# The pieces of x go to their partitions by DMA instead of by picks on the matrix engine

## The chip, the cores and the metric

One Trainium2 chip, one core of it. The metric is the device time of one launch in microseconds (us). The kernel before was timed three times, and once more under the profiler. TensorE (PE) multiplies, VectorE (DVE), ScalarE (ACT) and GpSimd (POOL) work on tiles in the on-chip memory, and SP issues most DMAs.

## The reference, cut to what matters

`x` is 64 x 64 x 512 (batch, time, features), the initial state `cond` 64 x 512. A GRU runs over the 64 time steps, and a feed-forward layer in emulated 8-bit floats follows.

```
def cell(h, x):
    gi = x @ W_ih + b_ih
    gh = h @ W_hh + b_hh
    i_r, i_z, i_n = jnp.split(gi, 3, axis=-1)
    h_r, h_z, h_n = jnp.split(gh, 3, axis=-1)
    r = jax.nn.sigmoid(i_r + h_r)
    z = jax.nn.sigmoid(i_z + h_z)
    n = jnp.tanh(i_n + r * h_n)
    h_new = (1.0 - z) * n + z * h
    return (h_new, h_new)
...
t = jax.nn.silu(g) * u
qt, st, sct = _reorder_quantize_x(t, down_reorder_index)
y = _qlinear(qt, st, sct, w_down, down_reorder_index)
...
x = x + ffn(gru(cond, x))
```

The recurrence is very sensitive to rounding in its first steps, so the kernel computes these with sums in an emulated order.

## The kernel before

**Stages.** A set-up splits the weights into half-precision kinds and writes them to DRAM (`w_rows`), to about 203 us of the span. Six *emulated* steps follow, to about 2,270 us, and then 58 plain steps with the feed-forward layer.

**Products.** The emulated steps are a list, `PRODUCTS`, of ten products (t, m): m = 0 is x of step t times W_ih, m = 1 the state times W_hh. The order is (0,0), (0,1), (1,0), (1,1), (2,0), (2,1), (3,0), (3,1), (4,1), (5,1); i is the place in it. Each has 32 blocks (`NBK`) of 16 rows of the contraction. For t < 2 a product is *fine* (`fine_chain`, 384 matmuls of 32 columns a block, two buffers, `PAIR`), after that a *sum* product (`sum_chain`, 64 matmuls a block, four buffers, `BUFS`). All of a product is added in the banks `run[m]`; `run_ok[1]` counts the blocks done, and with it everyone knows which buffer is free (`emptied`).

**What a product needs.** VectorE cuts the turned operand into six kinds of pieces (`cut_pieces`, into `a_split`). TensorE *picks* (L967): matmuls with the selection matrices `low_sel` and `whole_sel` bring rows of `a_split` to the partitions where the chain wants them, 8 groups of 10 matmuls in a fine product and of 8 in a sum product. ScalarE (`place`) and VectorE (`place_second`) copy the results into `low_a` and `whole_a`, one buffer for x and state alike. From these GpSimd (`one_hots`, L741 and L747), or ScalarE in (2,0) and (3,0) (`x_one_hots`, L833), makes a block's operands `whole_hot` and `low_hot`. SP loads a block's weights (`weights`, L687 and L694): 4 DMAs, in a fine product 12. In a fine product VectorE and ScalarE also rebase `whole_w` between blocks (L1047, L815), and for block 0 set it to zero (L1040, L822).

**Order around the change.** On TensorE a product is: in a state product the turn of the state (L948), two matmuls that clear `run[m]` (L955), the picks, then the chain. In an x product the cut was made during the state product ahead of it. SP waits before `weights(i)` until all blocks of the product before are done:

```
sp.wait_ge(run_ok[1], block_no(i, 0) + BUFS)
blocks(sp, i, load)
```

VectorE runs `elementwise(t - 1)`, the gates of the last step, during x product (t,0): in (1,0) woven between its rebasing, ten instructions a block, in (2,0) and (3,0) in one go. All loops of SP, GpSimd and ScalarE over blocks have one body for `bufs(i)` blocks, so two or four.

Of the kernel before, what the change touches and what calls it, by code (L numbers as in the profile page):

```python
# [11 lines left out]
F16 = mybir.dt.float16  # L12
# [71 lines left out]
def build(nc, x, cond, w_ih, w_hh, b_ih, b_hh, w_gate, w_up, w_down, up_idx, dn_idx, out):  # L84
# [14 lines left out]
    with ctx:  # L99
# [37 lines left out]
        with ExitStack() as ex:  # L137
# [112 lines left out]
            with ExitStack() as sx:  # L250
# [23 lines left out]
                id_z = ssem("id_z")  # L274
# [28 lines left out]
                with nc.Block() as block:  # L303
# [29 lines left out]
                    @block.gpsimd  # L333
                    def _(pool):
                        nc.gpsimd.memset(ex_ident[:], 0.0).then_inc(id_z, 1)
                        pool.wait_ge(id_z, 1)
# [46 lines left out]
                    def _(v):  # L383
# [18 lines left out]
                        v.wait_ge(id_ok, 1)  # L402
# [82 lines left out]
                    @block.tensor  # L485
                    def _(pe):
                        pe.wait_ge(id_ok, 1)
# [24 lines left out]
                        pe.wait_ge(plain_ok, 2)  # L512
                        x_pairs(pe, range(SETUP_PAIRS), raw, SETUP_BANKS)

            with ExitStack() as sx:
# [8 lines left out]
                low_a = ssb("low_a", [P, NBK, SUBS, B], F16)  # L524
                whole_a = ssb("whole_a", [P, NBK, B], F16)
# [9 lines left out]
                w_x = ssb("w_x", [P, KD, G3])  # L535
                COUNT_AT = 2
# [21 lines left out]
                placed_second = ssem("placed_second")  # L558
                w_in = [ssem(f"w_in{b}") for b in range(BUFS)]
# [35 lines left out]

                def places(i):

                    return 2 * PB if fine(i) else PB

# [24 lines left out]
                def blocks(eng, i, block, first=0):  # L624

                    for c in range(first):
                        block(c, c % bufs(i))
                    with eng.Fori(first // bufs(i), NBK // bufs(i)) as n:
                        for b in range(bufs(i)):
                            block(n * bufs(i) + b, b)  # L630
# [13 lines left out]
                with nc.Block() as block:  # L644
                    @block.sync
                    def _(sp):
# [29 lines left out]
                        def weights(i):  # L676
                            m = PRODUCTS[i][1]

                            def load(c, buf):

                                sp.wait_ge(run_ok[1], emptied(i, c))
# [16 lines left out]
                            sp.wait_ge(run_ok[1], block_no(i, 0) + BUFS)  # L698
                            blocks(sp, i, load)
# [27 lines left out]
                    def _(pool):  # L727
# [3 lines left out]
                        def one_hots(i):  # L731
                            m = PRODUCTS[i][1]

                            def make(c, buf):

                                pool.wait_ge(placed[m], placed_by(i) + placed_for(i, c))
                                pool.wait_ge(placed_second, second_by(i) + placed_for(i, c))
                                pool.wait_ge(hot_ok, block_no(i, c) + 1)
                                pool.wait_ge(run_ok[1], emptied(i, c))
                                if fine(i):  # L740
                                    nc.gpsimd.tensor_tensor(  # L741
                                        whole_hot[:, buf].rearrange("p s k c -> p (s k) c"),
                                        whole_a[:, bass.ds(c, 1), :].to_broadcast([P, 2 * BK, B]),
                                        whole_mask[:].rearrange("p s k -> p (s k)").unsqueeze(2).to_broadcast([P, 2 * BK, B]),
                                        ALU.mult).then_inc(whole_ok, 1)
                                    pool.wait_ge(whole_ok, block_no(fine_no(i), c) + 1)
                                nc.gpsimd.tensor_tensor(  # L747
                                    low_hot[:, buf].rearrange("p (s k) b -> p s k b", s=SUBS),
                                    low_a[:, bass.ds(c, 1), :, :].rearrange("p a s b -> p (a s) b").unsqueeze(2).to_broadcast([P, SUBS, SK, B]),
# [3 lines left out]
                            blocks(pool, i, make, FIRST)  # L753
# [14 lines left out]
                    def _(a):  # L768
                        for part in range(2):
                            own = slice(part * B, part * B + Q)  # L770
                            for bq in range(2):
                                nc.scalar.activation(whole_a[own, :, bq * Q:(bq + 1) * Q], ex_ident[own, own].unsqueeze(1).to_broadcast([Q, NBK, Q]),
                                                     ACT.Copy, scale=HIGH_ONE)
# [21 lines left out]
                        def place(i):  # L795
                            m = PRODUCTS[i][1]
                            for n in range(places(i)):
                                a.wait_ge(selected[m], placed_by(i) + n + 1)
                                group, whole = pick_of(i, n)
                                if whole:  # L800
                                    last = nc.scalar.activation(whole_a[Q:2 * Q, group::PB, :], picked(n, slice(Q, 2 * Q)), ACT.Copy)
                                else:
                                    for part in range(2):
                                        last = nc.scalar.activation(low_a[part * B:(part + 1) * B, group::PB, 0, :], picked(n, slice(0, B)), ACT.Copy)  # L804
# [21 lines left out]
                        def x_one_hots(i):  # L826
                            def make(c, buf):

                                a.wait_ge(placed_second, second_by(i) + places(i))
                                a.wait_ge(hot_ok, block_no(i, c) + 1)  # L830
                                a.wait_ge(run_ok[1], emptied(i, c))
                                for k in range(SK):
                                    last = nc.scalar.activation(low_hot[:, buf, k::SK, :],  # L833
                                                                low_a[:, bass.ds(c, 1), :, :].rearrange("p a s b -> p (a s) b"),
# [3 lines left out]
                            blocks(a, i, make)  # L838

                        for i, (t, m) in enumerate(PRODUCTS):  # L840
# [12 lines left out]
                    def _(pe):  # L853
# [97 lines left out]
                        def pick(i):  # L951
                            t, m = PRODUCTS[i]
                            need(pe, gates_ok[m], t * 2)
                            for u in range(2):
                                nc.tensor.matmul(run[m][u], zeros[:], zero_row[:], start=True, stop=True, skip_group_check=True)  # L955
                            pe.wait_ge(a_split_ok[m], t + 1)
# [38 lines left out]
                    def _(v):  # L995
# [3 lines left out]
                        def cut_pieces(t, m):  # L999
# [7 lines left out]
                            v.wait_ge(turned[m], t + 1)  # L1007
                            yield link(vs(a_rest[:, m], ps_a_both[m].rearrange("p (j s b) -> p s j b", j=2, s=2),
# [17 lines left out]
                        def place_second(i):  # L1026
                            m = PRODUCTS[i][1]
                            for n in range(places(i)):
                                v.wait_ge(selected[m], placed_by(i) + n + 1)
                                group, whole = pick_of(i, n)  # L1030
                                if whole:
                                    last = nc.vector.tensor_copy(whole_a[B + Q:2 * B, group::PB, :], picked(n, slice(B + Q, 2 * B)))
                                else:
                                    for part in range(2):
                                        last = nc.vector.tensor_copy(low_a[part * B:(part + 1) * B, group::PB, 1, :], picked(n, slice(B, 2 * B)))  # L1035
# [368 lines left out]
        with ExitStack() as sx:  # L1404
# [14 lines left out]
            ident_z = ssem("ident_z")  # L1419
# [23 lines left out]
            with nc.Block() as block:  # L1443
# [15 lines left out]
                def _(pool):  # L1459
                    nc.gpsimd.memset(ident[:], 0.0).then_inc(ident_z, 1)  # L1460
                    pool.wait_ge(ident_z, 1)
# [13 lines left out]
                def _(v):  # L1475
                    nc.vector.memset(zero16[:], 0.0).then_inc(zero_ok, 1)
                    v.wait_ge(ident_ok, 1)
# [723 lines left out]
```

## Time and profile before

| | us |
|---|---|
| timed runs | 3220.37, 3244.61, 3233.75 |
| their median | 3233.75 |
| the profiled execution | 3218.36 |
| its span | 3216.5 |
| mean granted clock of TensorE | 0.944 |

The span is the time between the first and the last instruction of the profiled execution. The profile has busy time by engine, the span in 40 slices (one is 80.4 us), DMA queues, the chain of work that ended last, and groups of instructions by line. A timeline row gives the start in us from the span's start, the duration, engine, line, operation, output and inputs, count, and in brackets the idle time of the engine before it and what ended that. `PEld` is TensorE loading weights, `SPq` a DMA issued by SP. Matmuls overlap, so the duration of one is far above its share.

### The profile page before, as it was taken

Reading aid. Unit: us, or ns where it says so; the run is one execution under the profiler, and the core shown is the slowest. Engines: PE = TensorE matmul, PEld = TensorE weight load, DVE = VectorE, ACT = ScalarE, POOL = GpSimd, SP = SyncE. Lnnn points to the kernel's source line nnn. Section 1 sums busy time; section 2 is a strip of 40 time slices with the busy share of each in tenths; the row PEclk is TensorE's granted clock in tenths of the full one; section 3 lists DMA queues with packets and bytes.
Section 4 is the critical chain, followed back from the end, with each engine's and each line's share of the span. In section 5 each row is a group of like instructions: output and inputs, shape, how many; then the busy total and the mean of one; then the engine's idle time right before and its main releaser. Section 6 shows DMA issues by size and latency. Waiting matters only on the chain. (4 is left out here: it accounts for less than half of the span.)

```text
span 3216.5 us, 156784 instructions
## 1 busy us (share of the span) xinstructions
PE 2801.9 (87%) x67963; PEld 1888.0 (59%) x67963; DVE 1808.8 (56%) x3503; ACT 1176.6 (37%) x2417; POOL 1249.5 (39%) x640
## 2 busy tenths in 40 slices
PE   5649999999999899999999999999941599999996
PEld 2227886888678677887767764646410244444442
DVE  6533423342369842523757427081767488888887
ACT  2332212222212122223806413030245377777774
POOL 1226554565455445553060341606020133333333
PEclk9869999999999999999999999999965799999998
DMA  6752222222122122222544452424240223222321
GB/s 173 173 145 65 62 65 54 60 66 62 50 59 59 53 61 53 63 62 66 151 135 123 123 146 79 141 102 122 88 153 25 92 78 91 85 83 84 90 72 48
DMA packets 214339, 286.43 MB, mean 89 GB/s; under 512 B 49197, under 2 KB 174151, under 8 KB 214023
## 3 DMA queue, kind: packets, MB, share of 16 engines
q1 hardware_dynamic: 194791, 235.99, 26.4%
q10 hardware_dynamic: 13568, 33.56, 2.9%
q0 software_dynamic: 5856, 15.22, 2.4%
q8 instruction: 78, 1.28, 0.2%
q14 instruction: 46, 0.38, 0.0%
HBM read 226.10 MB, written 58.48 MB: 88 GB/s over the span
## 5 line engine op out<-in xcount | busy, mean ns | idle before, releaser
L865 PE MATMUL psum<-whole_w,whole_hot 64*32 64x384 f16 x32768 | 1199.6, 325 | 38.5 <-issue 16.3
L873 PE MATMUL psum<-low_w,low_hot 64*32 64x384 f16 x16384 | 1004.1, 325 | 3.8 <-issue 3.8
L865 PEld LDWEIGHTS psum<-whole_w,whole_hot 64*32 64x32 f16 x32768 | 741.6, 93 | 192.6 <-DVE whole_w L1047 51.2
L747 POOL TENSOR_TENSOR low_hot<-low_a,sum_mask 128x1024 f16<-128x1024 f16 x256 | 485.2, 1895 | 537.7 <-DVE low_a L1035 434.0
L741 POOL TENSOR_TENSOR whole_hot<-whole_a,whole_mask 128x2048 f16<-128x2048 f16 x128 | 462.4, 3612 | 570.4 <-PE psum L865 502.9
L1047 DVE TENSOR_SCALAR whole_w<-psum 32x384 f16<-32x384 f32 x496 | 272.2, 549 | 691.9 <-PE psum L865 683.7
L815 ACT ACTIVATE whole_w<-psum 32x384 f16<-32x384 f32 x496 | 239.3, 483 | 960.3 <-PE psum L865 957.4
L935 PE MATMUL psum<-low_w,low_hot 64*64 64x384 f16 x12288 | 506.6, 324 | 9.5 <-ACT low_hot L833 7.9
L935 PEld LDWEIGHTS psum<-low_w,low_hot 64*64 64x64 f16 x12288 | 374.9, 108 | 140.3 <-ACT low_hot L833 8.4
L873 PEld LDWEIGHTS psum<-low_w,low_hot 64*32 64x32 f16 x16384 | 404.9, 93 | 59.2 <-issue 8.5
L1822 PE MATMUL psum<-wh,hT 128*64 128x256 f32 (+1 forms) x1856 | 315.0, 492 | 0.0
L2017 POOL TENSOR_TENSOR store<-store 128x512 f32<-128x512 f32 (+1 forms) x96 | 156.4, 1658 | 337.7 <-ACT store L1938 337.6
L231 PE MATMUL psum<-w_x,x_cols 128*64 128x256 f32 (+1 forms) x1408 | 237.0, 496 | 7.4 <-ACT x_cols L201 7.4
L1822 PEld LDWEIGHTS psum<-wh,hT 128*64 128x64 f32 x1856 | 128.9, 138 | 181.4 <-issue 156.2
L1843 PE MATMUL psum<-qgu,store 128*128 128x512 f16 (+1 forms) x768 | 173.1, 370 | 36.4 <-DVE store L2087 28.3
L1093 DVE SCALAR_TENSOR_TENSOR ex_gates_h<-psum,unscale,bias 128x384 f32<-128x384 f32 x12 | 7.0, 615 | 312.8 <-PE psum L935 297.8
L231 PEld LDWEIGHTS psum<-w_x,x_cols 128*64 128x64 f32 x1408 | 100.7, 139 | 137.6 <-issue 107.7
L833 ACT ACTIVATE low_hot<-low_a,sum_scale 128x128 f16 x512 | 156.6, 388 | 9.3 <-DVE low_a L1035 1.1
L195 ACT ACTIVATE psum<-bias_sum 128x512 f32<-128x512 f32 x58 | 34.8, 600 | 284.9 <-DVE ex_gates_h L1093 251.4
L1843 PEld LDWEIGHTS psum<-qgu,store 128*128 128x128 f16 x768 | 69.5, 99 | 116.5 <-issue 26.6
L804 ACT ACTIVATE low_a<-psum 64x256 f16<-64x256 f32 x160 | 60.2, 376 | 200.1 <-PE psum L967 195.5
L1566 PE MATMUL psum<-ident,q 128*128 128x128 f16 x132 | 18.8, 309 | 117.7 <-DVE q L1502 117.7
(265 smaller groups left out, 3126.2 us busy)
## 6 DMA issues: line engine op xcount, KB each, us to landing
low_w<-w_rows SPq DMA_DIRECT2D x384, 144.0 KB, 2.4
low_w<-w_rows SPq DMA_DIRECT2D x256, 120.0 KB
whole_w<-w_rows SPq DMA_DIRECT2D x1024, 24.0 KB, 1.8
x_gates<-x_out ACTq DMA_DIRECT2D x58, 384.0 KB, 2.4
xg<-x_gates SPq DMA_DIRECT2D x58, 384.0 KB, 3.2
low_w<-w_rows SPq DMA_DIRECT2D x256, 72.0 KB
low_w<-w_rows SPq DMA_DIRECT2D x384, 48.0 KB, 2.2
w_rows<-w_split SPq DMA_DIRECT2D x64, 144.0 KB
```

Of the source, the lines that this page charges most:

```text
L231: last = nc.tensor.matmul(banks[1][n % 2][part][half * B:(half + 1) * B, :], lhs, parts(w, k, half)[part], start=False, stop=True, skip_gr ...
L741: nc.gpsimd.tensor_tensor(whole_hot[:, buf].rearrange("p s k c -> p (s k) c"), whole_a[:, bass.ds(c, 1), :].to_broadcast([P, 2 * BK, B]), ...
L747: nc.gpsimd.tensor_tensor(low_hot[:, buf].rearrange("p (s k) b -> p s k b", s=SUBS), low_a[:, bass.ds(c, 1), :, :].rearrange("p a s b -> p ...
L815: last = nc.scalar.activation(whole_w[u * B:u * B + Q, buf, 1, bq, :], run[m][u][(2 + bq) * Q:(3 + bq) * Q, :], ACT.Copy, scale=1.0 / HIGH ...
L833: last = nc.scalar.activation(low_hot[:, buf, k::SK, :], low_a[:, bass.ds(c, 1), :, :].rearrange("p a s b -> p (a s) b"), ACT.Copy, scale= ...
L865: last = nc.tensor.matmul(run[m][u][j * Q:(j + 1) * Q, :], whole_hot[rows[u], buf, sign, kk, j % 2 * Q:(j % 2 + 1) * Q], whole_w[rows[u], ...
L873: nc.tensor.matmul(run[m][u][j * Q:(j + 1) * Q, :], low_hot[rows[u], buf, kk, j % 2 * Q:(j % 2 + 1) * Q], low_w[rows[u], buf, at:at + UC], ...
L935: last = nc.tensor.matmul(run[m][u][half * B:(half + 1) * B, :], low_hot[own, buf, kk, :], low_w[own, buf, at:at + UC], start=False, stop= ...
L1047: last = nc.vector.tensor_scalar(whole_w[u * B:u * B + Q, c % PAIR, 0, bq, :], run[m][u][bq * Q:(bq + 1) * Q, :], 1.0 / HIGH_ONE, None, AL ...
L1822: last = nc.tensor.matmul(dst, lhs, w, start=False, stop=True, skip_group_check=True)
L1843: last = nc.tensor.matmul(dst[:, 0:w], qhT[:, k, :], qgu[:, k, base + o:base + o + w], start=k == 0, stop=k == KD - 1)
L2017: nc.gpsimd.tensor_tensor(t_t[:, s], u_t[:, s], silu_t[:, s], ALU.mult).then_inc(t_ok, 1)
```

## The change

The x products of steps 1 to 3 get no picks and no copies. Their pieces are written to DRAM (`x_pieces`) and read from there into the partitions, by DMA, while the state product ahead of them runs: in (0,1) and (1,1) by SP, with the write ahead of the last eight blocks' weights and the reads spread over these; in (2,1) by ScalarE at its start. `low_a` and `whole_a` exist twice, for x and for the state, and their layout has the group outside. The picks of (0,0) and of all state products stay.

Three things go with it. SP's wait for the whole product ahead is replaced by a wait for each buffer (`opened`). The loops over blocks have one body for eight (`PB`) blocks. Two semaphores of the identity matrices are merged into others.

```diff
+                def regrouped(i):
+                    return i > 0 and bufs(i) != bufs(i - 1)
+
+                def opened(eng, i, c):
+                    eng.wait_ge(run_ok[1], emptied(i, c))
+                    if regrouped(i) and isinstance(c, int) and c < PAIR:
+                        eng.wait_ge(run_ok[1], block_no(i, 0) + BUFS - PAIR + 1 + c)
+
+                def by_dma(i):
+                    t, m = PRODUCTS[i]
+                    return m == 0 and t > 0
+
                 def places(i):
+                    if by_dma(i):
+                        return 0
                     return 2 * PB if fine(i) else PB
+
+                def pieces_of_x(t):
+                    t_fine = t < X_FINE
+                    kinds = LOW_ROWS if t_fine else SUM_ROWS
+                    low = [(part * B + row * SK, kind, None) for part in range(2) for row, kind in enumerate(kinds)]
+                    whole = [(part * B + Q + (sub * WHOLE_KINDS + row) * SK, kind, sub)
+                             for part in range(2) for sub in range(SUBS) for row, kind in enumerate(WHOLE_ROWS)]
+                    return low + whole if t_fine else low
+
+                def move_x(eng, piece):
+                    to, kind, sub = piece
+                    if sub is None:
+                        eng.dma_start(low_a[0][to:to + SK].rearrange("k q s g b -> k (q s) (g b)"),
+                                      x_pieces[kind].rearrange("(n k) c -> k n c", k=SK)).then_inc(moved_x, 16)
+                    else:
+                        eng.dma_start(whole_a[0][to:to + SK].rearrange("k q g b -> k q (g b)"),
+                                      x_pieces[kind].rearrange("(q s k) c -> s k q c", s=SUBS, k=SK)[sub]).then_inc(moved_x, 16)
+
+                def put_x(eng, t):
+                    eng.wait_ge(a_split_ok[0], t + 1)
+                    need(eng, moved_x, moved_by(t - 1))
+                    eng.dma_start(x_pieces[:].rearrange("j p c -> p j c"),
+                                  a_split[:, :, 0:KD, :].rearrange("p j g b -> p j (g b)")).then_inc(put, 16)
+                    eng.wait_ge(put, 16 * t)
...
-                        for b in range(bufs(i)):
-                            block(n * bufs(i) + b, b)
+                        for b in range(PB):
+                            block(n * PB + b, b % bufs(i), n, b)
...
-                            sp.wait_ge(run_ok[1], block_no(i, 0) + BUFS)
-                            blocks(sp, i, load)
+                            if not pieces:
+                                blocks(sp, i, load, 1 if regrouped(i) else 0)
+                                return
+                            blocks(sp, i, load, end=KD - 1)
+                            put_x(sp, t + 1)
+                            for c in range(NBK - PB, NBK):
+                                load(c, c % bufs(i), c // PB, c % PB)
+                                for piece in pieces[c % PB * share:(c % PB + 1) * share]:
+                                    move_x(sp, piece)
...
                             elif m == 0:
-                                a.wait_ge(placed[0], placed_by(i) + places(i))
                                 x_one_hots(i)
+                            elif t + 1 < X_SUMS:
+                                a.wait_ge(hot_ok, block_no(i, 0) + 1)
+                                put_x(a, t + 1)
+                                for piece in pieces_of_x(t + 1):
+                                    move_x(a, piece)
...
                                 nc.tensor.matmul(run[m][u], zeros[:], zero_row[:], start=True, stop=True, skip_group_check=True)
+                            if by_dma(i):
+                                return
```

On TensorE, between the chain of (0,1) and that of (1,0), the program before stands so (`low_sel` and `whole_sel` are the selection matrices):

```order
L897 COMPARE_AND_BRANCH
L955 MATMUL psum<-zero_row,zeros 128x384 x2
L967 MATMUL psum<-a_split,low_sel 128x256 x8
L967 MATMUL psum<-a_split,whole_sel 128x256 x2
...
L967 MATMUL psum<-a_split,whole_sel 128x256 x2
L897 UNCONDITIONAL_BRANCH
L897 ISA
L906 ISA
L865 MATMUL psum<-whole_w,whole_hot 32x384 x4
```

and that of the change so:

```order
L964 REGISTER_ALU
L964 COMPARE_AND_BRANCH
L1022 MATMUL psum<-zero_row,zeros 128x384 x2
L964 UNCONDITIONAL_BRANCH
L964 ISA
L973 ISA
L932 MATMUL psum<-whole_w,whole_hot 32x384 x4
```

Of the work between the chains only the two clears are left; at (2,0) and (3,0) it is the same.

On SP, in (0,1), from the end of its loop over 24 blocks on, the program of the change has:

```order
L678 COMPARE_AND_BRANCH
L646 DMA x_pieces<-a_split 128x6x256
L739 DMA low_w<-w_rows 40x2x768
L739 DMA low_w<-w_rows 24x2x768
L746 DMA whole_w<-w_rows 16x2x384 x4
L739 DMA low_w<-w_rows 40x2x768
L739 DMA low_w<-w_rows 24x2x768
L746 DMA whole_w<-w_rows 16x2x384 x4
L636 DMA low_ax<-x_pieces 8x16x256 x3
```

The write of the pieces stands ahead of block 24's weights, and three reads stand behind each block's twelve DMAs.

## Rows read from the trace of the kernel before

**Rows 1.** The page: busy time by engine; instruction queues: packets, MB

```profile
PE 2801.9 (87%) x67963; PEld 1888.0 (59%) x67963; DVE 1808.8 (56%) x3503; ACT 1176.6 (37%) x2417; POOL 1249.5 (39%) x640
...
q8 instruction: 78, 1.28, 0.2%
```

**Rows 2.** Timeline, start of (1,0): start us, us, engine, line, operation, tiles, count, idle before

```profile
846.97 0.50 PE L955 MATMUL psum<-zero_row,zeros 128*128 128x384 f16 x2
...
847.72 0.89 DVE L1040 MEMSET whole_w<- 32x384 uint32 x2
...
859.17 1.89 ACT L822 ACTIVATE whole_w<-zero_row 32x384 f16<-32x384 f16 x4
...
860.31 0.34 PE L865 MATMUL psum<-whole_w,whole_hot 64*32 64x384 f16 x4 [2.12 <-ACT whole_w L822]
```

**Rows 3.** Timeline, start of (2,0)

```profile
1511.26 7.15 PE L967 MATMUL psum<-a_split,low_sel 128*128 128x256 f16 x64
...
1522.35 1.17 PE L935 MATMUL psum<-low_w,low_hot 64*64 64x384 f16 x11 [3.94 <-ACT low_hot L833]
```

**Rows 4.** Timelines, start of (3,0) and its end

```profile
1705.90 5.31 PE L935 MATMUL psum<-low_w,low_hot 64*64 64x384 f16 x69 [1.34 <-issue]
...
1711.47 7.15 PE L967 MATMUL psum<-a_split,low_sel 128*128 128x256 f16 x64
...
1722.55 0.86 PE L935 MATMUL psum<-low_w,low_hot 64*64 64x384 f16 x8 [3.93 <-ACT low_hot L833]
...
1807.31 0.20 PEld L948 LDWEIGHTS psum<-ex_ident,a_in 128*128 128x128 f32 x2 [0.30 <-issue]
```

**Rows 5.** Windows: us, busy time and instructions of each engine, granted clock, DMA share, GB/s

```profile
861.00:871.00 10.00, 10.00 (x372) 8.25 (x364) 0.97 (x2) 1.02 (x3) 0.50 (x1) 0.83 0.02 5
1522.00:1532.00 10.00, 9.65 (x176) 7.08 (x180) 10.00 (x27) 9.46 (x32) 0.00 (x0) 0.72 0.19 57
1704.00:1716.00 12.00, 10.42 (x128) 7.55 (x121) 4.45 (x10) 3.01 (x8) 0.00 (x0) 1.00 0.23 50
1722.00:1732.00 10.00, 9.45 (x200) 7.19 (x204) 10.00 (x28) 9.47 (x32) 0.00 (x0) 0.83 0.23 66
```

**Rows 6.** Timelines of SP's queue (fine, start of (2,0), set-up); page: DMA issues to landing

```profile
791.66 0.79 SPq L687 DMA_DIRECT2D low_w<-w_rows  x2
...
800.92 0.79 SPq L687 DMA_DIRECT2D low_w<-w_rows  x2
...
804.80 1.79 SPq L694 DMA_DIRECT2D whole_w<-w_rows  x4
...
1511.35 9.75 SPq L687 DMA_DIRECT2D low_w<-w_rows  x16
...
58.04 117.48 SPq L308 DMA_DIRECT2D w_rows<-w_split  x48
...
low_w<-w_rows SPq DMA_DIRECT2D x384, 48.0 KB, 2.2
```

**Rows 7.** Timeline, ScalarE's one-hots in (2,0)

```profile
1519.77 15.35 ACT L833 ACTIVATE low_hot<-low_a,sum_scale 128x128 f16 x48 [0.56 <-DVE low_a L1035]
```

**Rows 8.** Timelines: ScalarE's start; VectorE's gates at the end of (2,0)

```profile
203.36 1.06 ACT L772 ACTIVATE whole_a<-ex_ident 32x1024 f16<-32x1024 f32 x1 [17.03 <-PEq L303]
...
216.30 0.76 ACT L804 ACTIVATE low_a<-psum 64x256 f16<-64x256 f32 x2 [8.93 <-PE psum L967]
...
1608.31 1.14 DVE L1093 SCALAR_TENSOR_TENSOR ex_gates_x<-psum,unscale,bias 128x384 f32<-128x384 f32 x2 [15.20 <-PE psum L935]
```

**Rows 9.** Timeline, GpSimd's one-hots in (1,0)

```profile
1083.20 3.60 POOL L741 TENSOR_TENSOR whole_hot<-whole_a,whole_mask 128x2048 f16<-128x2048 f16 x1 [3.85 <-PE psum L865]
1086.98 1.89 POOL L747 TENSOR_TENSOR low_hot<-low_a,sum_mask 128x1024 f16<-128x1024 f16 x1 [0.17 <-POOL whole_hot L741]
...
1125.28 3.61 POOL L741 TENSOR_TENSOR whole_hot<-whole_a,whole_mask 128x2048 f16<-128x2048 f16 x1 [4.68 <-PE psum L865]
```

**Rows 10.** DMA queues over 1080 to 1115: instruction packets, MB

```profile
q8 instruction: 9, 0.15, 2.0%
```

More of the change, by code:

```diff
@@ L535, in build @@
                 w_x = ssb("w_x", [P, KD, G3])
+                x_pieces = nc.dram_tensor("x_pieces", [A_KINDS, P, KD * B], F16, kind="Internal").ap()
                 COUNT_AT = 2
@@ L622, in emptied, with blocks @@
                     return block_no(i, c) + BUFS - bufs(i) + 1
[L624 to L628, printed above, removed]
-                        for b in range(bufs(i)):
-                            block(n * bufs(i) + b, b)
+                def blocks(eng, i, block, first=0, end=KD):
+                    for c in range(first * PB):
+                        block(c, c % bufs(i), c // PB, c % PB)
+                    with eng.Fori(first, end) as n:
+                        for b in range(PB):
+                            block(n * PB + b, b % bufs(i), n, b)
                 def placed_for(i, c):
@@ L676, in weights, with load @@
                         def weights(i):
-                            m = PRODUCTS[i][1]
-                            def load(c, buf):
-                                sp.wait_ge(run_ok[1], emptied(i, c))
+                            t, m = PRODUCTS[i]
+                            pieces = pieces_of_x(t + 1) if fine(i) and m == 1 and t + 1 < X_SUMS else ()
+                            share = -(-len(pieces) // PB)
+                            def load(c, buf, gk, group):
+                                opened(sp, i, c)
                                 src = w_rows[bass.ds(c + m * NBK, 1)].rearrange("a r n -> r (a n)")
@@ L731, in one_hots, with make @@
                         def one_hots(i):
[L732 to L737, printed above, removed]
+                            t, m = PRODUCTS[i]
+                            def make(c, buf, gk, group):
+                                if by_dma(i):
+                                    pool.wait_ge(moved_x, moved_by(t))
+                                else:
+                                    pool.wait_ge(placed[m], placed_by(i) + placed_for(i, c))
+                                    pool.wait_ge(placed_second, second_by(i) + placed_for(i, c))
                                 pool.wait_ge(hot_ok, block_no(i, c) + 1)
-                                pool.wait_ge(run_ok[1], emptied(i, c))
+                                opened(pool, i, c)
                                 if fine(i):
@@ L748, in make @@
                                     low_hot[:, buf].rearrange("p (s k) b -> p s k b", s=SUBS),
-                                    low_a[:, bass.ds(c, 1), :, :].rearrange("p a s b -> p (a s) b").unsqueeze(2).to_broadcast([P, SUBS, SK, B]),
+                                    low_a[m][:, group, :, bass.ds(gk, 1), :].rearrange("p s a b -> p (s a) b").unsqueeze(2).to_broadcast([P, SUBS, SK, B]),
                                     sum_mask[:].unsqueeze(1).unsqueeze(3).to_broadcast([P, SUBS, SK, B]),
                                     ALU.mult).then_inc(hot_ok, 1)
-                            blocks(pool, i, make, FIRST)
+                            blocks(pool, i, make, 0 if by_dma(i) else 1)
                         for i, (t, m) in enumerate(PRODUCTS):
@@ L800, in place @@
                                 if whole:
[L801 removed]
+                                    last = nc.scalar.activation(whole_a[m][Q:2 * Q, group, :, :], picked(n, slice(Q, 2 * Q)), ACT.Copy)
                                 else:
                                     for part in range(2):
[L804 removed]
+                                        last = nc.scalar.activation(low_a[m][part * B:(part + 1) * B, group, 0, :, :], picked(n, slice(0, B)), ACT.Copy)
                                 last.then_inc(placed[m], 1)
@@ L826, in x_one_hots, with make @@
                         def x_one_hots(i):
-                            def make(c, buf):
-                                a.wait_ge(placed_second, second_by(i) + places(i))
+                            def make(c, buf, gk, group):
+                                a.wait_ge(moved_x, moved_by(PRODUCTS[i][0]))
                                 a.wait_ge(hot_ok, block_no(i, c) + 1)
-                                a.wait_ge(run_ok[1], emptied(i, c))
+                                opened(a, i, c)
                                 for k in range(SK):
                                     last = nc.scalar.activation(low_hot[:, buf, k::SK, :],
-                                                                low_a[:, bass.ds(c, 1), :, :].rearrange("p a s b -> p (a s) b"),
+                                                                low_a[0][:, group, :, bass.ds(gk, 1), :].rearrange("p s a b -> p (s a) b"),
                                                                 ACT.Copy, scale=sum_scale[:, k:k + 1])
                                 last.then_inc(hot_ok, 1)
-                            blocks(a, i, make)
+                            blocks(a, i, make, 1 if regrouped(i) else 0)
                         for i, (t, m) in enumerate(PRODUCTS):
```

38 lines of the change are left out of this document (22 added, 16 removed).

## The prediction

> **What bounds the kernel now.** I read the page first. TensorE is busy 87% of the span, VectorE 56%, the others less [rows 1], so I take TensorE's matmul chains as the bound of the emulated steps, and what can be won there is time in which no chain runs. Next I read the timeline at the three places where the change takes the picks out, the starts of products (1,0), (2,0) and (3,0).
>
> - (1,0) [rows 2]: the two clears start at 846.97, the picks follow, and the chain starts at 860.31. Its last releaser is ScalarE's zero of `whole_w` (L822), which stands behind its copies of the picks.
> - (2,0): picks from 1511.26 for 7.15 us and the chain at 1522.35 after 3.94 us idle [rows 3]; ScalarE, which copies first, starts the one-hots only at 1519.77 [rows 7].
> - (3,0) [rows 4]: picks from 1711.47, chain at 1722.55, the same shape.
>
> At the starts of the state products the picks cannot go (they wait for the new state), and the change leaves them. Last I read the windows for the granted clock [rows 5], because after the idle ahead of each of these chains it falls: 0.83 over 861 to 871, 0.72 over 1522 to 1532, 0.83 over 1722 to 1732.
>
> **The change, part by part.** *Picks removed.* What could hold the new chain start?
>
> (1,0): run banks are cleared at once. The first base needs VectorE's memset, which starts at 847.72 right behind the gate values and takes 0.89 for two [rows 2], so the first is there at about 848.17. ScalarE's zeros no longer have copies ahead of them and lie under the last block. From the end of two zeros (859.17 + 0.94 = 860.11) to the chain (860.31) is 0.20. So the chain could start at 848.37 instead of 860.31: **11.94 us**. It needs block 0's one-hots and weights by then. GpSimd takes 3.6 + 1.9 = 5.5 us for a block [rows 9], SP 5.7 us to issue (800.92 to 806.59) and the last DMA some 2.2 us to land [rows 6], 7.9 in all; both may start when block 30 of the product before is done, one block, 9.26 us, ahead of the end (SP's rhythm: 791.66, 800.92). Covered, by 1.4 us. Block 1's have the whole of block 0.
>
> (2,0): no base is needed. The chain could start where the first pick did, 1511.26, instead of 1522.35: **11.09 us**. ScalarE makes a block in 8 x 0.32 = 2.6 us (48 in 15.35, [rows 7]) and has block 0's one-hots and SP its weights during the last fine block. Block 1 is late: its buffer was in use by the last fine block, so SP opens it at about 1511.0, its four DMAs go out as block 0's did from 1511.35, at 0.6 each (16 in 9.75, [rows 6]), the fourth at about 1513.1, and lands 2.2 later, 1515.3 to 1515.4. TensorE wants it at 1511.26 + 2.65 = 1513.9 (product (3,0) runs 32 blocks from 1722.55 to 1807.31, [rows 4]). A new wait of **1.5 us**; blocks 2 and 3 follow at 2.4 us each and are in time. Net 9.6.
>
> (3,0): four buffers before and after, so everything for blocks 0 to 3 is loaded and made during the last four blocks of (2,1). 1711.47 instead of 1722.55: **11.08 us**.
>
> *Clock.* The shortfalls of [rows 5] are 0.17 x 10 + 0.28 x 10 + 0.17 x 10 = 6.2 us of work at full clock. They go if the idle that came before them goes. What is left is 0.9 us at (1,0) and 1.5 at (2,0). The nearest row is an idle of 1.34 us that ended at 1705.90 [rows 4], after which the clock over 1704 to 1716 stayed 1.00. I take the whole **6.2**; the other end is 1.7, (3,0) alone, which has no idle left.
>
> *DMAs added.* In (0,1) SP writes `x_pieces` once ahead of its last eight blocks, waits for it, and issues 24 moves, three a block; in (1,1) 16, two a block; in (2,1) ScalarE issues 16, which has nothing else to do there between its copies and the next product. In a fine product SP has 9.26 - 5.7 = 3.6 us free a block. The lower end of an issue is 0.4 us (two in 0.79, [rows 6]): 1.2 a block, hidden by that idle. The upper end is the writes of the set-up, 48 in 117.48 or 2.45 each, with their waits for VectorE in it [rows 6]: three make 7.35, 3.8 too late a block. A move has 128 or 64 short rows, near `low_w` (40x2 and 24x2) and `whole_w` (16x2) in kind and far from the set-up, where SP waits for VectorE's splitting; so I take 0.4 and nothing. The write moves 384 KB. At the 2.2 us of a load it is there as block 24 opens, since SP reaches it 5.7 us after block 21's end and has 3.6 left: nothing, and up to 2 us once a product if its many short rows take twice that. The last move of (0,1) is issued behind block 31's weights: that block opens 18.5 us ahead of the end, so 18.5 - 5.7 - 1.2 = 11.6 ahead, and at 2.2 us to land the pieces are there 9.4 ahead, where GpSimd may start at 9.26 and has 3.8 us to spare.
>
> *Copies moved.* `low_a` is laid out by group; the one-hot instructions keep count and size, so nothing. Four more 1 us activations at the start (L772, four from 203.36 on) end before 212, ScalarE's first copy is at 216.30 [rows 8]: hidden by the wait for the pieces. `elementwise` in (2,0) starts earlier by the copies that VectorE loses, about 7 us, while the chain ends some 11 earlier: the 15.20 us that VectorE waited at its end [rows 8] shrink by 4, and nothing waits for it. VectorE's weave in (1,0), which stretches that product, is unchanged.
>
> Sum: 11.94 + 9.6 + 11.08 + 6.2 = **38.8 us**. The profiled execution took 3218.36, so 3179.6 on its terms. The three timed ones were 3220.37, 3244.61 and 3233.75, median 15.4 above it; the mean of the four is 3229.3. I forecast on the mean: 3229.3 - 38.8 = 3190.5, say **3190**. On the median it would be 3195.
>
> **Code loading** is the term I can't place. In (1,0) GpSimd's whole one-hots, one a block, start at 1083.20 and, three blocks on, at 1125.28 [rows 9] where 9.26 apart is the rule: 42.1 us, 14.3 lost, and in that stretch nine packets of instructions were loaded on TensorE's queue [rows 10], of 78 in the whole span [rows 1]. It happened in mid-loop, where the code had been there before. The change moves all code behind (0,1), so this may vanish (3176) or come twice (3205); both ends go into the range.
>
> The Trainium skill (Runtime: NRT & Kernel Launch, Instruction fetch mechanics) says that a taken branch to code outside a small window must fetch it first, and gives 32 KiB as the store of most engines. The row that bears on it: 78 instruction packets, 1.28 MB, for TensorE's 135,926 instructions [rows 1], under ten bytes each, so most trips of the loops loaded nothing. By the rule taken strictly, loops of eight blocks could load each trip; by the row, they don't. This is the last rival below.
>
> **Rivals.**
> 1. *Forecast*, 0.62: the three heads go.
> 2. *The head is hidden behind something else*, 0.18: the first block's weights, one-hots or code are late at each new start. For it: the cover at (1,0) is 1.4 us. If each start waits 4 us and the clock falls as before: 11.94 + 9.6 + 11.08 - 12 + 0 = 20.6 saved, 3209. Within 1%.
> 3. *SP is late in the state products*, 0.14: moves at 2.45. Then 3.8 x 8 in (0,1) and (2 x 2.45 - 3.6) x 8 = 10.4 in (1,1), 40.8 lost, 3231. Within 1%. It decides from 1.2 us an issue on. Against it: SP's issues are even throughout these stretches.
> 4. *Slower*, 0.06: the loops of SP, GpSimd and ScalarE, two or four blocks long and now eight, load code on each trip. SP makes 4 + 3 + 4 + 3 = 14 trips in fine products. At the 14.3 us that one reload of TensorE's cost, 200 - 38.8 = 161 more, 3390. It decides from (38.8 + 32.3) / 14 = 5.1 us a trip. Against it: [rows 1] as above.
>
> **How the numbers follow.** Within 1% (32.3 us of 3233.75) is about what a measurement of this kernel can tell from no change; faster means below 3201.4. Rival 1 has its ends at 3176 and 3205, of which about one part in ten lies above the bound; rival 2 may land either side with the executions' own spread of 24 us. Faster 0.60, same 0.34, slower 0.06. The range is from 3166 (no reload, on the profiled execution's terms: 3179.6 - 14.3 = 3165.3) to 3219 (rival 2's 3209 and ten of the executions' 24 us).
>
> **What would show it.** No `low_sel` or `whole_sel` matmul between the clears and the chain at the three places; the first chain matmul within 1.5 us of the clears; a wait of about 1.5 us at block 1 of (2,0); clock 1.00 in the first 10 us of (3,0); SP's weight issues 9.26 apart in the last eight blocks of (0,1). Wrong: blocks of GpSimd's more than 9.5 apart there, idle of TensorE over 2 us at the new starts, or many more instruction packets than 78 on TensorE's queue or SP's rhythm broken at a loop's turn.

## The result, and the profile after

The changed kernel takes 3183.05 us, median of four runs (3173.21 to 3186.78), against 3228.12 for the kernel before (four runs, 3220.37 to 3244.61): ratio 0.9849, 95% interval 0.9802 to 0.9896, or 45 us less. The forecast was 3190 (3166 to 3219). The profiled execution took 3183.72, 34.6 less than the profiled one before. The medians below leave out three executions that lay in the slow state: 4285.13 us of before_padded, 3254.72 and 6509.78 us of after_padded87.

The page of the changed kernel, as in [rows 1]:

```profile
span 3181.9 us, 155502 instructions
...
PE 2773.8 (87%) x67755; PEld 1877.9 (59%) x67755; DVE 1784.3 (56%) x3447; ACT 1159.3 (36%) x2365; POOL 1247.0 (39%) x640
...
q8 instruction: 67, 1.10, 0.1%
```

The 208 picks and 56 copies of VectorE are gone, and 11 packets of code of the queue q8 (which I take for TensorE's: nine of them come while its loop stands still), of which more below. The starts of the three products are in the timeline of the changed kernel, against [rows 2 to 4]:

```profile
846.56 0.50 PE L1022 MATMUL psum<-zero_row,zeros 128*128 128x384 f16 x2
...
847.31 0.89 DVE L1111 MEMSET whole_w<- 32x384 uint32 x2
...
847.79 0.34 PE L932 MATMUL psum<-whole_w,whole_hot 64*32 64x384 f16 x4 [0.73 <-DVE whole_w L1111]
...
1487.08 0.50 PE L1022 MATMUL psum<-zero_row,zeros 128*128 128x384 f16 x2
...
1487.50 2.79 PE L1002 MATMUL psum<-low_w,low_hot 64*64 64x384 f16 x64
1491.23 4.06 PE L1002 MATMUL psum<-low_w,low_hot 64*64 64x384 f16 x93 [0.94 <-issue]
...
1685.64 0.50 PE L1022 MATMUL psum<-zero_row,zeros 128*128 128x384 f16 x2
...
1686.07 2.14 PE L1002 MATMUL psum<-low_w,low_hot 64*64 64x384 f16 x48
```

The chain follows its clears by 1.2 us in (1,0), where it waits for VectorE's memset, and by 0.4 in the others; in (2,0) block 1 waits 0.94 for its weights. The windows behind the three starts, against [rows 5], have the full clock:

```profile
848.00:858.00 10.00, 8.80 (x367) 7.04 (x363) 1.30 (x3) 0.97 (x2) 4.32 (x2) 1.00 0.23 59
1487.00:1497.00 10.00, 9.06 (x214) 7.02 (x214) 9.69 (x33) 9.48 (x32) 0.00 (x0) 1.00 0.55 152
...
1686.00:1696.00 10.00, 10.00 (x245) 7.16 (x248) 9.89 (x33) 8.94 (x30) 0.00 (x0) 1.00 0.52 147
```

To see where the time went I took the times between the first clears of successive products, from the timelines of all traces (us; "rest" is all behind the clears of (5,1)). These stretches differ between executions too, "rest" by up to 9 us over all traces:

| trace | to (0,0) | (0,0) | (0,1) | (1,0) | (1,1) | (2,0) | (2,1) | (3,0) | (3,1) | (4,1) | rest |
|---|---|---|---|---|---|---|---|---|---|---|---|
| before | 209.8 | 320.3 | 316.9 | 343.3 | 320.6 | 97.6 | 102.7 | 96.5 | 181.6 | 180.9 | 1046.5 |
| changed | 211.5 | 319.6 | 315.4 | 320.2 | 320.3 | 85.2 | 113.4 | 84.0 | 182.0 | 181.1 | 1049.2 |

Three stages pay: (1,0) -23.1, (2,0) -12.4, (3,0) -12.5. Everything else is within 3 us but (2,1), which is **10.7 longer**. The trace shows why. ScalarE's queue, TensorE, and the windows there:

```profile
1595.80 0.40 ACTq L646 DMA_DIRECT2D x_pieces<-a_split  x1
1599.83 14.22 ACTq L636 DMA_DIRECT2D low_ax<-x_pieces  x16
```

```profile
1589.75 18.53 PE L1002 MATMUL psum<-low_w,low_hot 64*64 64x384 f16 x452
1613.70 6.57 PE L1002 MATMUL psum<-low_w,low_hot 64*64 64x384 f16 x120 [5.42 <-issue]
```

```profile
1598.00:1603.00 5.00, 5.00 (x132) 3.60 (x124) 4.86 (x9) 0.00 (x0) 3.79 (x2) 1.00 0.99 228
1603.00:1608.00 5.00, 5.00 (x132) 3.54 (x124) 4.89 (x6) 0.00 (x0) 3.78 (x2) 1.00 1.05 139
1608.00:1613.00 5.00, 0.28 (x8) 0.00 (x0) 4.89 (x7) 0.00 (x0) 1.89 (x1) 1.00 1.09 129
1613.00:1618.00 5.00, 4.30 (x72) 3.05 (x76) 4.89 (x7) 0.00 (x0) 0.00 (x0) 0.66 0.57 127
```

Two windows of (2,1) in the kernel before, for comparison:

```profile
1625.00:1660.00 35.00, 35.00 (x868) 25.22 (x864) 34.02 (x45) 0.00 (x0) 24.72 (x13) 1.00 0.49 139
1660.00:1711.00 51.00, 49.42 (x1168) 34.98 (x1156) 0.31 (x2) 0.00 (x0) 28.51 (x16) 1.00 0.51 124
```

The sixteen reads of step 3's pieces go out at once, the DMA engines are full (share about 1.0, where the stage before had 0.5), TensorE stops 5.42 us, for which the profile names no releaser, and comes back at a clock of 0.66. A second stop of 2.23 us ends at 1,628.02. The two stops and the clock (0.34 x 5 = 1.7) are 9.4 of the 10.7. The DMA view of 1,598 to 1,613, then the page's issues over the whole kernel, show weights that land late:

```profile
low_w<-w_rows SPq DMA_DIRECT2D x11, 144.0 KB, 4.4
```

```profile
low_w<-w_rows SPq DMA_DIRECT2D x384, 144.0 KB, 2.5
```

A load of 144 KB lands 4.4 us after its issue instead of 2.5, and a block of a sum product lasts 2.6. That is the median; the load that TensorE needed was later still. In the trace's semaphore records TensorE's queue waits from 1,607.50 for 6.14 us, and one of its two conditions is the semaphore of that block's weights. SP had issued these from 1,600.96 to 1,602.47, and their last landing stands at 1,613.61, 11 us after the last issue. The stop ends at 1,613.70.

### The profile page after: what moved, and what is told of

It reads as the page before. It is cut to its first block and busy times, and to the rows that moved or that the text cites. A ratio compares the mean times of both kernels' runs of the same rounds, so it can differ in the third digit from the quotient of the medians.

```text
span 3181.9 us, 155502 instructions
## 1 busy us (share of the span) xinstructions
PE 2773.8 (87%) x67755; PEld 1877.9 (59%) x67755; DVE 1784.3 (56%) x3447; ACT 1159.3 (36%) x2365; POOL 1247.0 (39%) x640
## 5 line engine op out<-in xcount | busy, mean ns | idle before, releaser
L809 POOL TENSOR_TENSOR low_hot<-low_ah,sum_mask 128x1024 f16<-128x1024 f16 x192 | 363.7, 1894 | 514.6 <-DVE low_ah L1106 411.1
L1002 PEld LDWEIGHTS psum<-low_w,low_hot 64*64 64x64 f16 x12288 | 383.4, 107 | 132.3 <-issue 12.4
L803 POOL TENSOR_TENSOR whole_hot<-whole_ah,whole_mask 128x2048 f16<-128x2048 f16 x64 | 231.1, 3610 | 274.2 <-PE psum L932 237.0
L803 POOL TENSOR_TENSOR whole_hot<-whole_ax,whole_mask 128x2048 f16<-128x2048 f16 x64 | 231.1, 3611 | 270.2 <-PE psum L932 256.1
L896 ACT ACTIVATE low_hot<-low_ax,sum_scale 128x128 f16 (+1 forms) x512 | 156.6, 388 | 104.9 <-PE psum L1002 85.8
L809 POOL TENSOR_TENSOR low_hot<-low_ax,sum_mask 128x1024 f16<-128x1024 f16 x64 | 121.3, 1895 | 10.3 <-POOL whole_hot L803 9.7
```

Source lines behind the costliest of these rows:

```text
L803: nc.gpsimd.tensor_tensor(whole_hot[:, buf].rearrange("p s k c -> p (s k) c"), whole_a[m][:, group, bass.ds(gk, 1), :].to_broadcast([P, 2 ...
L809: nc.gpsimd.tensor_tensor(low_hot[:, buf].rearrange("p (s k) b -> p s k b", s=SUBS), low_a[m][:, group, :, bass.ds(gk, 1), :].rearrange("p ...
L896: last = nc.scalar.activation(low_hot[:, buf, k::SK, :], low_a[0][:, group, :, bass.ds(gk, 1), :].rearrange("p s a b -> p (s a) b"), ACT.C ...
L1002: last = nc.tensor.matmul(run[m][u][half * B:(half + 1) * B, :], low_hot[own, buf, kk, :], low_w[own, buf, at:at + UC], start=False, stop= ...
```

## The experiments

The first four ran on one chip with the kernel before (3226.75 us there), the next four on one (3229.04), the last four on one (3222.47).

**after_again** is the changed kernel once more.

> The changed kernel once more, as the yardstick of this chip and for a second trace. In its first trace product (2,1), from its clears to those of (3,0), took 113.7 us where the kernel before took 102.9, and TensorE sat idle 5.4 us at 1,608. Theory A (ScalarE's burst of sixteen reads takes the DMA engines from the weights, share 1.0 over 1,598 to 1,613): the same stretch takes 112 to 115 us again, with the idle within 10 us of the burst. Theory B (chance, like a code load): it takes about 103. Product (1,0) took 320.0 us from clears to the turn of (1,1), before 343.0, of which 14.3 was a code load in mid-loop: if that load is chance by execution, (1,0) may take 334 here; if it belongs to the layout of the code, 320 again.

3183.97 us, ratio 0.9863 (0.9803 to 0.9922). (2,1) took 110.7, a little under the 112 expected, with the stop again behind the burst. The burst began 7 us later this time, and the stop 9:

```profile
1606.62 14.41 ACTq L636 DMA_DIRECT2D low_ax<-x_pieces  x16
...
1622.43 7.79 PE L1002 MATMUL psum<-low_w,low_hot 64*64 64x384 f16 x152 [4.77 <-issue]
```

The queue waits here from 1,616.48 for 5.90 us; the last landing of the block's weights stands at 1,622.34. Chance (B) is out. (1,0) took 325.5, between the two values expected, but again with 6 packets of code: the reload of [rows 9, 10] doesn't come back.

**paced** spreads the burst.

```diff
-                                for piece in pieces_of_x(t + 1):
+                                for n, piece in enumerate(pieces_of_x(t + 1)):
+                                    a.wait_ge(hot_ok, block_no(i, 4 + 3 * n // 2) + 1)
                                     move_x(a, piece)
```

> The changed kernel with the sixteen reads of (2,1) paced: one for each block and a half, each behind a wait for GpSimd's one-hots of block 4 + 3n/2, instead of all in one go. Theory A (the burst starves the weights): (2,1) takes 103 to 105 us instead of 113.7, (3,0) starts as early as now, and the kernel is 9 to 11 us faster than the changed one, near 3172. Theory C (the 16 reads cost DMA time however they are spread, since the weights need 0.6 of the engines already): (2,1) takes 109 or more. Theory B (chance): no difference.

3176.39 us, ratio 0.9853 (0.9792 to 0.9914); (2,1) took 106.4, and its longest stop in the chain is 0.8 us. Both are short of what was expected (103 to 105, near 3172). The burst is the cause of 4 to 7 us. Up to 3.7 are left over the stage before, and the DMA share over the spread reads is 0.76:

```profile
1604.31 48.79 ACTq L636 DMA_DIRECT2D low_ax<-x_pieces  x16
```

```profile
1618.00:1660.00 42.00, 41.66 (x1020) 36.31 (x1016) 9.14 (x14) 0.00 (x0) 30.13 (x17) 1.00 0.76 170
```

**x3_picks** gives step 3 its picks back, so (2,1) has no moves.

```diff
-                    return m == 0 and t > 0
+                    return m == 0 and 0 < t < 3
...
-                            elif t + 1 < X_SUMS:
+                            elif t + 1 < X_SUMS - 1:
```

> The changed kernel with step 3's pieces picked on TensorE again, so no DMA in (2,1); steps 1 and 2 as changed. Theory A: (2,1) falls back to about 103 (-10.8) and (3,0) rises from 83.8 to 96 less its wait (+12.4, of which up to 1.5 is clock), so the kernel comes out within 2 us of the changed one: the third move of the change pays nearly nothing as it is written. If the moves of step 3 were worth their 12.4 in full (theory B), it is 12 us slower.

3183.36 us, ratio 0.9867 (0.9808 to 0.9925), the changed kernel's time. (2,1) is back at 104.9, (3,0) at 98.2. The two stages together take 203.1, in the three traces of the changed kernel 197.4, 194.7 and 197.1. So step 3's moves, as they are written, win 12 to 14 us in (3,0) and lose about half of that in (2,1); what is left, 6 to 8 us by the stages, the kernel's medians (four executions each, 13 to 15 us apart) don't show.

**no_moves** keeps all picks; early opening, loops of eight blocks and doubled tiles stay.

```diff
-                    return m == 0 and t > 0
+                    return False
...
-                            pieces = pieces_of_x(t + 1) if fine(i) and m == 1 and t + 1 < X_SUMS else ()
+                            pieces = ()
...
-                            elif t + 1 < X_SUMS:
+                            elif False:
```

> Nothing of x goes by DMA: all picks stay. What is left of the change are the early opening of SP's buffers, the loops of eight blocks and the two pairs of tiles low_a and whole_a. If the whole gain is the three starts (theory A), this takes the time of the kernel before, 3228, within the spread of 12, less up to 14 if the code load in (1,0) of the kernel before goes away with the layout of the code. If the loops of eight or the early opening gain or lose by themselves, SP's issues or the fine blocks show it: more or less than 9.26 us a block.

3227.78 us, ratio 1.0014 (0.998 to 1.0048). The rest of the change is worth nothing by itself, within the interval (6 us faster to 15 slower), and its loops of eight cost nothing that shows. Its trace has the 78 packets of the kernel before, 15 of them in (1,0), which took 345.5.

**double** issues the sixteen reads a second time, into a spare tile.

```diff
                                 for piece in pieces_of_x(t + 1):
                                     move_x(a, piece)
+                                for to, kind, _ in pieces_of_x(t + 1):
+                                    a.dma_start(spare_a[to:to + SK].rearrange("k q s g b -> k (q s) (g b)"),
+                                                x_pieces[kind].rearrange("(n k) c -> k n c", k=SK)).then_inc(moved_x, 16)
```

> The changed kernel with the burst of (2,1) doubled: after its sixteen reads ScalarE issues the same sixteen again, into a tile that nobody reads. Theory A (the burst starves the weights of DMA time): (2,1), 113.4 and 110.7 us in two traces of the changed kernel, against 102.7 before, loses as much again, 119 to 124, with the idle of TensorE behind a burst twice as long. Rival (the loss is one stall for another reason, the write of the pieces or a code load at that point): 111 to 114 as now.

3190.03 us, ratio 0.9895 (0.9856 to 0.9934). (2,1) took 117.3, 4 to 7 us above the changed kernel's first two traces and 3 above the highest (114.5) of six traces with one burst. TensorE stops twice, as it did in the changed kernel's first trace (5.42 and 2.23):

```profile
1609.34 13.38 PE L1006 MATMUL psum<-low_w,low_hot 64*64 64x384 f16 x256 [6.24 <-issue]
1625.55 14.72 PE L1006 MATMUL psum<-low_w,low_hot 64*64 64x384 f16 x320 [2.83 <-POOL low_hot L810]
```

Both cases missed: 117.3 is above the rival's 111 to 114 and below the 119 to 124 of theory A. The loss grows little with the reads, and the two stops by 1.4 us together. One trace can't say more; doubling leaves the size of the effect open. That the reads are the cause rests on paced, x3_picks and the landing times.

**late_open** puts SP's old wait ahead of the x products.

```diff
+                            if by_dma(i):
+                                sp.wait_ge(run_ok[1], block_no(i, 0) + BUFS)
                             if not pieces:
```

> The changed kernel with SP's old wait in front of the x products of steps 1 to 3: their weights are opened only when the whole product before is done; the moves stay. Theory: the heads then last until block 0's weights are there. (1,0): 5.7 us of issues and 2.2 to land behind the clears, so the chain starts about 8 us behind them instead of 1.2, +6.5; (2,0) and (3,0): 1.9 + 2.2 against 0.3, +3.8 less the 1.2 that block 1 waits in (2,0) now; clock 1 to 3 us. Sum 13 to 16 us more, 3197 to 3200. If the weights are not what the head waits for, no difference.

3199.48 us, ratio 0.9903 (0.9873 to 0.9933): 15.5 us more than the changed kernel's 3184 (measured on another chip; by the ratios to the kernel before it is 13). From the clears to the chain it now takes 7.7 us at (1,0), and 4.3 and 5.0 at (2,0) and (3,0), against 1.2, 0.4 and 0.4; the last two stages took 89.6 and 91.1. At (1,0) the profile names the releaser, the DMA of `whole_w`. So picks gone and weights opened early is one change: either half alone leaves a head.

**after_padded** and **after_padded87** ask why (1,0) won 23 us where the start explains 12. They add one-column matmuls ahead of the chain of (1,0), 80 and 87.

```diff
                             if by_dma(i):
+                                for _ in range(80 if i == 2 else 0):
+                                    nc.tensor.matmul(run[m][0][:, 0:1], zeros[:], zero_row[:, 0:1], start=True, stop=True, skip_group_check=True)
                                 return
```

> The changed kernel with 80 matmuls of one column each ahead of the chain of (1,0), as many as the picks had there, so the code of that chain's loop lies where it lay in the kernel before. They add a zero to a cleared bank. In both traces of the changed kernel TensorE's queue loaded 6 packets of code in (1,0), in the kernel before and in the one without moves 15, nine of them in mid-loop at a loss of some 11 to 14 us. Theory D (the reload belongs to the place of the loop in the code): 15 packets here too, and (1,0) takes 320 to 325 plus 11 to 14 plus 2 to 4 for the 80 themselves, 333 to 343. Theory E (it belongs to the timing of the picks, or to chance): 6 packets and 322 to 329.

3190.35 us, ratio 0.9877 (0.9839 to 0.9915), 7 packets in (1,0), 327.1 us: no reload. One of the 7 comes at the product's end. Theory D as I had put it fell, but I had counted the picks' matmuls and not their 13 more semaphore instructions. Seven matmuls, 14 instructions, make up for these:

> The changed kernel with 87 one-column matmuls ahead of the chain of (1,0) instead of 80. With 80 there were 7 packets of code and no reload. Counting instructions, the trace has 16 semaphore instructions among the picks and 3 in their place here, so with 80 the loop lay 13 instructions short of its place in the kernel before; with 87 it lies 1 beyond that. A loop of a fine product has 1,549 instructions, that is 6.05 packets of 256 by the bytes of the packets and of the code; it touches seven packets, or eight where it starts in the last 13 instructions of one. Theory D' (reload where the loop touches eight): 15 packets or so in (1,0), nine in mid-loop, and 11 to 14 us more than with 80, near 3203. Theory E (place has nothing to do with it): 7 packets, near 3190.

3212.95 us, ratio 0.9953 (0.9923 to 0.9983), 23 us more than with 80 (on another chip; by the ratios about 25). The 87 take 0.2 us more than the 80. The DMA view of (1,0) in the kernel with 87, and in the kernel before:

```profile
q8 instruction: 33, 0.54, 0.8%
```

```profile
q8 instruction: 15, 0.25, 0.3%
```

In its trace nine packets came in mid-loop not once but three times, from 894, 992 and 1,046 us, each time just behind a turn of the loop, and (1,0) took 373.3. The place of the loop decides whether it can happen; that how often it does differs from execution to execution I infer from the spread of the times (3193 to 3237 us, and the 3255 left out), not from traces.

**before_padded** and **before_pad8** take the reload away from the kernel before, by 48 and by 8 such matmuls at TensorE's start, where it waits for x.

```diff
+                        for _ in range(8):
+                            nc.tensor.matmul(psum[:, 7, 0:1], zeros[:], zero_row[:, 0:1], start=True, stop=True)
                         turn(0, 0)
```

> The kernel before with 48 matmuls of one column at TensorE's start of the emulated steps, where it waits for x, so that all loops of its code lie 96 instructions further on. Theory D: the nine packets in mid-loop of (1,0) go away or move to another fine product; if they go everywhere, the kernel is 11 to 14 us faster, near 3215, with 67 to 69 packets in all instead of 78. Theory E: 15 packets in (1,0) and 343 us as before.

> The kernel before with only 8 one-column matmuls at TensorE's start, 16 instructions, while it waits for x. Theory D': 16 instructions carry the loop of (1,0) over the edge of a packet, so it touches seven again: 69 packets instead of 78, (1,0) 330 to 334 us instead of 343, the kernel 11 to 16 us faster than before, as with 48. Theory E' (the 48 helped by something else, such as the clock at the start): no change from before.

3212.30 us, ratio 0.9953 (0.9931 to 0.9975), and 3212.76, ratio 0.9972 (0.9951 to 0.9994). Both have 69 packets in all and 7 in (1,0), which took 333.4 and 337.7, the second above the 330 to 334 expected. Against the kernel before on the same chip the medians are 17 and 10 us less, the second a little under what was expected. So sixteen instructions that do nothing make the kernel before about 10 us faster, and narrower: ten runs from 3205 to 3218 where 23 of the kernel before went from 3206 to 3245.

**paced_again** and **after_third** compare the two on one chip.

> The paced kernel again, beside the changed one on the same chip, with more rounds. In its first trace (2,1) took 106.4 us against 113.4, 110.7 of the changed kernel and 102.7 of the one before, and no idle of TensorE over 2 us was left there. Theory A: 5 to 8 us faster than the changed kernel, ratio to before near 0.984.

> The changed kernel, the yardstick for the paced one: ratio to before 0.985 to 0.987, (2,1) 111 to 114 us.

3179.98 us, ratio 0.9861 (0.9828 to 0.9895), and 3183.64, ratio 0.9876 (0.9842 to 0.991). (2,1) took 103.5 and 112.3. The paced kernel is the fastest in both sets, by 7.6 and 3.7 us of medians, the second under the 5 to 8 expected; the intervals overlap, so the stage's 4 to 9 us is shown and the kernel's gain is only likely.

## Why the prediction was right, and where it was not

**The three starts: right.** (1,0): from clears to chain 13.34 us before, 1.23 after, 12.1 less for 11.94. (2,0): 12.4 less for 9.6 and 2.8 of clock. (3,0): 12.5 less for 11.08 and 1.7. The new wait in (2,0) was 0.94 for 1.5. For (1,0) the clock's 1.7 and the reload, below, come on top. late_open shows that the early opening was needed, as the step assumed.

**The clock: right.** 1.00 in the first ten us of all three.

**SP's moves: right.** The timeline of the changed kernel in (0,1):

```profile
796.20 1.05 SPq L636 DMA_DIRECT2D low_ax<-x_pieces  x3
800.36 0.68 SPq L739 DMA_DIRECT2D low_w<-w_rows  x2
...
809.62 0.68 SPq L739 DMA_DIRECT2D low_w<-w_rows  x2
```

Three cost 1.05 us, and blocks stay 9.26 apart. (0,1) took 315.4 against 316.9. The write landed in 2.8.

**The moves in (2,1): the step that failed.** I wrote that ScalarE "has nothing else to do there" and priced them at nothing. I had asked who issues, not who shares the transfer. SP's weights take half of the DMA engines' time there, four buffers ahead but 2.6 us a block. With the burst one block's weights landed 11 us after their last issue, where TensorE's queue asked for them after 5, and the stage lost 8 to 11 us. [rows 5] had no window of (2,1) but its last few us; one would have shown the share of 0.5 against 0.20 in (0,1), and the cover the fine product has and the sum product hasn't. paced and x3_picks settle it as the burst, and the landing times show the way. What the last 1 to 4 us in the paced (2,1) are stays open.

**Code loading: the term left open decided a quarter or so of the gain.** It vanished, as one of its two ends had it, and it was not chance: all eight traces with the moves and without padding have 6 packets in (1,0), both of the old layout (the kernel before and no_moves) 15. Its size was read too large. I held the three blocks of [rows 9] against 9.26 us each and got 14.3; but the trips of TensorE's loop that the reload fell in, the twelfth and thirteenth, took 32.8 + 18.4 us with it and 19.6 + 21.4 in the changed kernel without it. That is 10 us in the profiled execution. In the medians it is 10 and 17 (before_pad8, before_padded).

**The number: right by two errors that cancel.** The profiled pair has a gain of 34.6 us: the three heads with their clock 38 of the 38.8 forecast, the reload 10 more, the burst 11 less, and 3 that the other stages grew by. The medians give 45, since the profiled execution of the kernel before (3218.36) was one of its faster ones. So the likeliest case was right and its heads were right in size; that the total fell so near 3190 was luck, for neither the reload nor the burst was in the sum. Against the kernel before without its reload (3212.76, with the changed kernel at 3183.64 on the same chip), the change is worth about 29 us, 0.9%, not 45.

**The head hidden behind something else, SP late** (the second and third rival): both are out by the rows above, heads of 1.2 and 0.4 us and moves of 0.35 us each.

**The slower rival** (loops of eight load code on each trip) is out in its cost: no_moves has these loops and takes the time of the kernel before. The other instruction queue of the page, q14, does bring more code with them, 58 packets for 46 (60 in the changed kernel), but no time that shows.

## What to carry to other kernels

Work that is in the way at the start of a stage can go beside the stage ahead of it, if the buffers it needs open as early; check both. A transfer is hidden only if the DMA engines have room in that stage, whoever issues it: read the share of the window it goes to, and spread it. Where a loop nearly fills an engine's store of code (next section), a few instructions more or less ahead of it move the kernel by as much as a real change; count instruction packets before and after, and hold a change against a kernel of the same layout.

## What the runs showed of the hardware

A fine loop of TensorE has 1,549 instructions, counted in the trace: 768 pairs of weight load and matmul, eight semaphore instructions, five of registers and branch. The Trainium skill (Runtime: NRT & Kernel Launch, Instruction fetch mechanics) gives TensorE a store of 128 KiB, 2,048 instructions, filled in blocks of 16 KiB or 256. Such a loop touches seven blocks, or, in 12 of 256 places (not the 13 I wrote), eight, the whole store. The packets of the trace have that size (1.10 MB in 67). The runs agree. Counted from the loop's place in the kernel before, which has one reload, the same loop one instruction further on has three, and 13 and 173 instructions nearer the start (after_padded, the changed kernel) or 16 and 96 further on (before_pad8, before_padded) it has none. That an eighth block is the cause is thus borne out by six layouts, but I did not read the blocks' addresses. Why the reload comes in mid-loop, behind eleven of the sixteen trips in the kernel before and behind two, six and eight in after_padded87, stays open. A trip with a reload took 33 to 34 us, most without one 18 to 22.
